# Layer 3's later keys and values moved behind the context pass, and the context's normed rows made by ScalarE and GpSimd

## The chip, the cores and the metric

One core of one Trainium2 chip runs the whole program. The metric is the device time of one execution in microseconds (us). Engines: PE is TensorE (matmul), PEld its weight loads, DVE is VectorE, ACT is ScalarE, POOL is GpSimd, SP is SyncE, which here only issues DMAs. A PE clock of 1.00 in the profile is the upper of TensorE's two levels (2.4 GHz), 0.50 the lower (1.2 GHz); a value between them is a mean over a stretch.

## The reference

Four layers of cross-attention and feed-forward act on x (8 batches of 56 tokens, width 128). Every layer but layer 2 attends with keys and values made from the same context, 8 batches of 1500 rows of 128:

```python
x = x + tanh(g_xattn[0]) * L0_xattn(layernorm(x), ctx, ctx, mask, ...)   # linear attention, 16 heads
x = x + tanh(g_ffn[0])   * L0_ffn(layernorm(x), ...)                      # ternary weights, int8-like rows
x = x + tanh(g_xattn[1]) * L1_xattn(layernorm(x), ctx, ctx, ...)          # window of 64
x = x + tanh(g_ffn[1])   * L1_ffn(...)                                    # 16 + 2 experts
x = x + tanh(g_xattn[2]) * L2_xattn(ctx, layernorm(x), ...)               # keys and values of layer_norm(ctx, w, b)
x = x + tanh(g_ffn[2])   * L2_ffn(...)
x = x + tanh(g_xattn[3]) * L3_xattn(ctx, ctx, layernorm(x), Wv, Wk, Wq)   # ctx @ Wk.T, ctx @ Wv.T
x = x + tanh(g_ffn[3])   * L3_ffn(...)                                    # 8 experts
```

Layer 0 needs, of each context batch, normed keys and scaled values; layer 2 needs the context's rows with their mean taken off, divided by their deviation, times a weight plus a bias (`L2_xattn_ln_x_w`, `L2_xattn_ln_x_b`); layer 3 needs plain products of the context with two 128x128 matrices. 1500 rows are 125 partitions times 12 tiles.

## The kernel before, in words

Each engine has its own program, written out in the order in which it runs; semaphores order them against one another, nothing else does. The program has stages, one after another.

**The context pass** (to 254.7 us) is eight turns of `context(b, p, ...)`, one function of that name for PE, ACT and DVE, with buffers p = b % 2. In a turn PE makes the centred rows (`cT` times `w_c`, L684), layer 3's keys (L692), layer 0's keys and values (L701), layer 0's sums over the batch before (`l0_sums`, L663), layer 3's values (L713), layer 2's keys of the batch before, for their norms (`l2_keys`, L673), and the turned normed rows (L726). DVE takes the centred rows out of PSUM, times the reciprocal deviation plus the bias, into `cln` (L1730); it makes the lower half of layer 3's keys (float16 remainders), key features (`key_features`, L1696), the statistics of the next batch (`statistics`, L1710 to L1719), sums of squares (L1749), the scaled keys `kn`, and layer 2's norms (`l2_norms`, L1702). ACT squares and copies PSUM banks. POOL multiplies `kn` by a weight and adds a bias (L1443, L1444) and makes `rhs0` out of the loaded rows (L1448 to L1452). SP stores `cln`, its turned form, and layer 3's keys and values of every batch to HBM (`store_results`), and loads the batch after next once `rhs0` is made.

**The middle** (254.7 to 339.7 us) is layer 0's attention on the sums of the pass, its dense layer, its feed-forward and the queries of layer 1; it ends where DVE first reads layer 1's scores (`shift1(0)`). It is a chain of small steps. Where PE would idle, `keep_clock(n, bank)` (L645) issues n matmuls that nobody reads. DVE sums and rounds the five ternary weight matrices there (`weight_sums`, `quantised_weights`). A `layernorm` on DVE waits in its middle for POOL (`rsqrt`, L1462), which raises four numbers per row to the power -0.5.

**After it** come layer 1's attention and experts, layer 2 (460 to 615 us; POOL adds up probabilities at L1521 all along), its feed-forward, layer 3 and its experts. The change leaves their order alone except where it says so.

The helper `tt` on DVE is `tensor_tensor` and has line L1551 wherever it is called from.

```python
dve.tensor_scalar(kpr, kn, 0.0, 1e-6, ALU.max, ALU.add).then_inc(l0_kp, 1)   # key_features, L1696
```

## Time and profile before

| | us |
|---|---|
| three runs | 911.19, 912.78, 916.82 (median 912.78) |
| profiled execution | 915.11 |
| its span, first to last instruction | 913.5 |

The span holds the context pass (0 to 254.7), the middle (254.7 to 339.7), and the rest. In the page of the profile "busy" is the time in which an engine executed something; the timeline views give start and length of instructions that follow one another with one form (xN: so many), and in brackets the idle time before them with the engine that ended it. A length includes a wait that the engine makes after it has begun an instruction.

### The profile page before, as it was taken

How to read it: one execution, taken by the hardware profiler on the slowest of the kernel's cores; microseconds unless marked ns; L12 is line 12 of the kernel's file. 1: busy time of each engine (PE TensorE's matmuls, PEld its weight loads, DVE VectorE, ACT ScalarE, POOL GpSimd, SP SyncE). 2: the span in 40 equal slices, each digit the busy share in tenths (PEclk: the TensorE clock that was granted, in tenths of full speed). 3: DMA queues.
4: the chain of work that ended last, by engine and by line, in shares of the span. 5: the costliest groups of instructions: out<-in, count | busy, mean ns of one | idle time of the engine just before them, and what ended most of it. 6: DMA issues, size and time to landing. Idle time of an engine off the chain costs nothing.

```text
span 913.5 us, 16850 instructions
## 1 busy us (share of the span) xinstructions
PE 803.2 (88%) x5836; PEld 513.8 (56%) x5836; DVE 632.3 (69%) x1302; ACT 396.7 (43%) x650; POOL 278.0 (30%) x215
## 2 busy tenths in 40 slices
PE   4879998899877877899789999998889999988996
PEld 3757776677644435566345555555326656654665
DVE  4869989697779768465645566557788988806652
ACT  1556665566620203253344554540016766663341
POOL 2431344313413012045147777770050000000111
PEclk9889999899998898699989999999958998999999
DMA  6467766564232000020602242205804455500230
GB/s 187 153 223 250 262 218 198 200 202 162 85 120 21 1 1 1 1 74 32 160 1 71 85 120 74 70 0 69 167 2 117 123 135 156 156 2 24 70 104 22
DMA packets 46651, 94.03 MB, mean 103 GB/s; under 512 B 16698, under 2 KB 30010, under 8 KB 44274
## 3 DMA queue, kind: packets, MB, share of 16 engines
q1 hardware_dynamic: 46594, 93.25, 34.9%
q8 instruction: 38, 0.62, 0.3%
q14 instruction: 19, 0.16, 0.1%
HBM read 61.58 MB, written 31.65 MB: 102 GB/s over the span
## 4 chain that ended last, share of the span: by engine, by line
PE 38%; DVE 22%; issue 4%; ACT 3%; POOL 3%; DMA 1%; POOLq 0%; DVEq 0%; ACTq 0%
DVE arena L2099 9%; PE ps L997 8%; PE ps L987 6%; DVE arena L1551 4%; PE ps L930 2%; PE ps L1164 2%; PE ps L1174 2%; PE ps L1099 2%; PE ps L1088 2%; ACT arena L1382 2%; POOL arena L1521 2%; PE ps L943 1%; PE ps L1073 1%; POOL arena L1462 1%; PE ps L879 1%
## 5 line engine op out<-in xcount | busy, mean ns | idle before, releaser
L1551 DVE TENSOR_TENSOR arena<-ps,arena 128x448 f32<-128x448 f32 (+8 forms) x160 | 99.2, 641 | 65.3 <-ACT arena L1405 19.1
L2099 DVE TENSOR_REDUCE arena<-ps 112x1 f32<-112x500 f32 x192 | 115.6, 667 | 18.3 <-PE ps L1073 17.4
L1521 POOL TENSOR_TENSOR arena<-arena 125x448 f32<-125x448 f32 x96 | 108.8, 1133 | 26.3 <-ACT arena L1359 24.8
L1382 ACT ACTIVATE arena<-ps 125x896 f32<-125x896 f32 x96 | 87.0, 917 | 30.4 <-PE ps L1088 29.9
L997 PE MATMUL ps<-arena 125*128 125x448 f32 (+1 forms) x208 | 98.3, 554 | 1.3 <-ACT arena L1359 0.8
L1462 POOL TENSOR_TENSOR arena<-arena 112x4 f32<-112x4 f32 x11 | 11.3, 1025 | 287.5 <-DVE arena L1575 281.4
L1551 DVE TENSOR_TENSOR arena<-ps,rn 125x448 f32<-125x448 f32 x96 | 59.3, 618 | 51.3 <-PE ps L987 47.0
L1359 ACT ACTIVATE arena<-arena,kbias 125x448 f32<-125x448 f32 x96 | 63.7, 668 | 66.7 <-DVE arena L1551 46.3
L645 PE MATMUL ps<-w_k2h 128*128 128x512 f16 x376 | 88.7, 391 | 0.4 <-ACT arena L1285 0.4
L673 PE MATMUL ps<-w_k2h,arena 128*125 128x512 f16 x288 | 70.1, 401 | 12.5 <-ACT arena L1245 12.3
L987 PE MATMUL ps<-arena 128*125 128x448 f16 (+3 forms) x312 | 78.1, 360 | 3.0 <-DVEq L1562 3.0
L1443 POOL TENSOR_TENSOR arena<-arena,vec 125x1536 f32<-125x1536 f32 x8 | 27.7, 3458 | 154.9 <-DVE arena L1551 154.9
L987 PEld LDWEIGHTS ps<-arena 128*125 128x125 f16 (+1 forms) x312 | 40.8, 135 | 57.8 <-issue 42.6
L1702 DVE TENSOR_REDUCE rn<-arena 125x512 f32 (+1 forms) x96 | 61.0, 681 | 5.8 <-ACT arena L1213 5.8
L1213 ACT ACTIVATE arena<-ps 125x512 f32<-125x512 f32 x96 | 57.3, 597 | 16.8 <-PE ps L673 13.1
L645 PEld LDWEIGHTS ps<-w_k2h 128*128 128x128 f16 x376 | 37.5, 101 | 45.8 <-issue 7.4
L1496 POOL TENSOR_TENSOR arena<-arena 112x512 f32<-112x512 f32 x26 | 32.9, 1265 | 95.5 <-DVE arena L1551 95.1
L673 PEld LDWEIGHTS ps<-w_k2h,arena 128*125 128x125 f16 x288 | 40.7, 144 | 37.3 <-ACT arena L1245 13.6
L1073 PE MATMUL ps<-arena 64*112 64x500 f16 x192 | 55.2, 450 | 7.1 <-issue 4.3
L1099 PE MATMUL ps<-arena 125*32 125x168 f32 x768 | 51.9, 342 | 8.7 <-ACT arena L1382 8.3
L997 PEld LDWEIGHTS ps<-arena 125*128 125x128 f32 (+1 forms) x208 | 38.3, 192 | 14.0 <-issue 8.4
L1088 PE MATMUL ps<-arena 64*125 64x112 f16 x768 | 43.6, 242 | 0.0
(278 smaller groups left out, 1403.4 us busy)
## 6 DMA issues: line engine op xcount, KB each, us to landing
d_k<-arena SPq DMA_DIRECT2D x24, 375.0 KB
d_v<-arena SPq DMA_DIRECT2D x8, 1125.0 KB
arena<-d_k SPq DMA_DIRECT2D x96, 93.8 KB
arena<-d_v SPq DMA_DIRECT2D x8, 1008.0 KB
arena<-in_ctxT SPq DMA_DIRECT2D x8, 750.0 KB, 14.1
d_cln<-arena SPq DMA_DIRECT2D x8, 750.0 KB
d_clnT<-arena SPq DMA_DIRECT2D x8, 750.0 KB
arena<-d_clnT SPq DMA_DIRECT2D x8, 750.0 KB
```

The costliest lines, as they stand in the source:

```text
L645: pe.matmul(ps[0:D, k, :], w_k2h[:, 0, 0:D], w_k2h[:, 0, :], start=True, stop=True)
L673: mm = pe.matmul(ps[0:KP, k, :], clnT[p][:, a, KP * j:KP * j + KP], w_k2h[:, w, :], start=(n == 0), stop=(n == 2))
L987: mm = pe.matmul(ps[0:rows, (t + p) % 2, 0:N].rearrange("p (h q) -> p h q", h=H8), clnT_s[p][:, a, cols:cols + rows], qtT[:, q, :, bass.ds ...
L997: pe.matmul(ps[0:D, 4 + 2 * p, 0:N], cln_s[p][0:rows, t, :], pexp[(t + p) % 2][0:rows], start=(t == 0), stop=(t == KT)).then_inc(l2_pv, 1)
L1073: pe.matmul(ps[0:TT, max_bank(bn, u), 0:500], q.rearrange("p o h q -> p (o h q)"), kst[pn][64 * r:64 * r + 64, g, 500 * third:500 * third ...
L1088: mm = pe.matmul(ps[0:KP, 2 * (t % 2) + r, 112 * g:112 * g + 112], kst[p][rows, g, KP * t:KP * t + KP], qst3[rows, b:b + 1, g, 2 * r:2 * r ...
L1099: pe.matmul(ps[32 * g:32 * g + 32, 6, 0:168], v3s[p][:, t, 32 * g:32 * g + 32], p3[t % 2][:, 3 * g:3 * g + 3, :].rearrange("p h q -> p (h ...
L1359: act.activation(pexp[(t + p) % 2][0:rows], sscl[(t + p) % 2][0:rows], ACT.Exp, bias=bias)\
L1382: act.activation(p3[t % 2].rearrange("p (k h) q -> p k (h q)", k=2), ps[0:KP, 2 * (t % 2):2 * (t % 2) + 2, 0:8 * S], ACT.Exp).then_inc(l3_ ...
L1521: ins = pool.tensor_tensor(psum2[p][0:rows], psum2[p][0:rows], pexp[(t + p) % 2][0:rows], ALU.add)
L1551: return dve.tensor_tensor(out, a, b, op)
L2099: dve.tensor_reduce(mx3[bn % 2][:, u % 2, u % 8 // 2, u // 8:u // 8 + 1], ps[0:TT, max_bank_of(bn, u), 0:500], AX.X, ALU.max).then_inc(l3_ ...
```

## The change

It does eight things.

1. The centring product goes: `w_c`, its 12 matmuls a turn on PE and the 12 DVE instructions that read them. Instead ACT makes the normed rows from the loaded ones with 12 instructions of 125x128 (`rows`: a scale and a bias per row, which DVE's new `scales` makes), at the end of the turn before; POOL multiplies them by the weight and adds the bias (two 125x1536 instructions).
2. Of layer 3's keys and values each turn makes the first third (a "unit": 500 keys, 4 tiles of values). The other 16 units, numbered 8 to 23, are made in the middle: `later(...)` on PE and ACT, `remainders(...)` on POOL, `store_later` and `load_later` on SP.
3. POOL makes the keys' lower halves (`late_k` minus the upper half) and a second copy of the upper half. POOL's turn is now: normed rows, remainder, `rhs0`, `kn`.
4. Layer 0's query path (layernorm of x, product with `w_q0`, layernorm, turn) moves from the middle to the start of the program, as `query_rows`, `query_norm`, `query_columns`.
5. The last batch's layer 2 keys, squares and norms move from the end of the pass into the middle, into the time in which layer 0's attention is stored and loaded again.
6. The `keep_clock` calls of the middle are replaced by units, or go. Layer 0's hidden banks shrink from eight to six to make room.
7. Three of the five ternary matrices are rounded where all five were; the other two between the first two batches of layer 2.
8. The loops of the pass are written out. The loads of layer 2's weights and of the first experts come later; DVE waits for the last stores of units ahead of `shift1(0)`.

```diff
+UNITS = [(b, 0) for b in range(B)] + [(b, third) for b in (7, 6, 0, 1, 2, 3, 4, 5) for third in (1, 2)]
...
@@ SP @@
+            def store_later(u):
+                (b, third), h = UNITS[u], u % 3
+                sp.wait_ge(l_lo, u + 1)
+                sp.wait_ge(l_dup, u + 1)
+                sp.dma_start(k3_in[b, :, :, 500 * third:500 * third + 500], late_k3[h]).then_inc(st_l[h], 16)
...
@@ PE context @@
-                for u in range(3):
-                    k = bank_d(b, u)
-                    for j in range(4):
-                        mm = pe.matmul(ps[0:KP, k, D * j:D * j + D], cT[p][:, 4 * u + j, :], w_c,
-                                       start=True, stop=True)
...
+                later_keys(cT[p][:, 0:4, :], bank_a(b, 6)).then_inc(a_full, 1)
+                later_values(cT[p][:, 0:4, :], bank_a(b, 7)).then_inc(a_full, 1)
...
@@ PE middle @@
+            def later(*units):
+                for u in units:
...
+                    if u > B:
+                        pe.wait_ge(lk_taken, u - B)
+                    later_keys(tiles, 6).then_inc(lk_full, 1)
+                    if u > B:
+                        pe.wait_ge(lv_taken, u - B)
+                    later_values(tiles, 7).then_inc(lv_full, 1)
...
-            keep_clock(45, 3)
+            later(10, 11)
+            pe.wait_ge(l0_att, 1)
+            l2_keys(B, 1, 0, bank=3)
...
@@ ACT @@
+            def take_later(u, k, keys, values):
...
+                if u:
+                    act.wait_ge(l_lo, u)
+                act.wait_ge(*keys)
+                act.copy(late_k3[h][:, 0, :], ps[0:D, k[0], 0:500])
+                act.copy(late_k, ps[0:D, k[0], 0:500]).then_inc(keys_taken(u)[0], 1)
...
+            def rows(b, p, loads):
+                act.wait_ge(st[p], 32 * loads)
+                act.wait_ge(c_rstd, b + 1)
+                for j in range(KT):
+                    ins = act.activation(cln[p][:, j, :], c_in[p][:, j, :], ACT.Identity, bias=sm[:, 12, j:j + 1],
+                                         scale=sm[:, 6, j:j + 1])
+                ins.then_inc(c_rows, 1)
...
@@ POOL @@
+            def remainders(*units):
+                for u in units:
+                    k3 = late_k3[u % 3]
+                    pool.wait_ge(*keys_taken(u))
+                    pool.tensor_tensor(k3[:, 1, :], late_k, k3[:, 0, :], ALU.subtract).then_inc(l_lo, 1)
+                    pool.tensor_copy(k3[:, 2, :], k3[:, 0, :]).then_inc(l_dup, 1)
+
+            for b in range(B):
+                p = b % 2
+                pool.wait_ge(c_rows, b + 1)
+                ch.link(pool.tensor_tensor(cln[p], cln[p], spread("L2_xw", KP, KT), ALU.mult))
+                pool.tensor_tensor(cln[p], cln[p], spread("L2_xb", KP, KT), ALU.add).then_inc(c_ready, 1)
+                remainders(b)
+                pool.wait_ge(l0_w, b + 1)
+                pool.wait_ge(acc_full, b + 1)
+                ch.step(pool.tensor_copy(rhs0[:, :, D:D + 1], em[:, b, :].unsqueeze(2)))
+                ch.step(pool.tensor_copy(rhs0[:, :, D + 1:D + 2], em2[:, b, :].unsqueeze(2)))
+                pool.tensor_tensor(rhs0[:, :, 0:D], c_in[p], sm[:, 11, 0:KT].unsqueeze(2)
+                                   .broadcast_to([KP, KT, D]), ALU.mult).then_inc(l0_rhs, 1)
+                pool.wait_ge(l0_kn, b + 2)
+                ch.link(pool.tensor_tensor(kn, kn, spread("L0_g", KP, KT), ALU.mult))
+                pool.tensor_tensor(kn, kn, spread("L0_b", KP, KT), ALU.add).then_inc(l0_kaff, 1)
...
@@ DVE @@
+            def scales(b):
+                dve.wait_ge(c_sd, b + 1)
+                ch.link(dve.reciprocal(sm[:, 6, 0:KT], sm[:, 5, 0:KT]))
+                tt(sm[:, 12, 0:KT], sm[:, 3, 0:KT], sm[:, 6, 0:KT], ALU.mult).then_inc(c_rstd, 1)
...
-                for j in range(KT):
...
-                    ins = dve.scalar_tensor_tensor(cln[p][:, j, :], ps[0:KP, 3 + j // 4, D * (j % 4):D * (j % 4) + D],
...
-                    tt(k_lo[p][:, 500 * u:500 * u + 500], ps[0:D, 3 + u, 0:500],
-                       k_hi[p][:, 500 * u:500 * u + 500], ALU.subtract).then_inc(d_free, 1)
...
+            for h in range(3):
+                dve.wait_ge(st_l[h], 32 * 8)
             shift1(0)
...
             batch2(0, 0, first=True)
+            quantised_weights((3, 4))
             batch2(1, 1)
```

What the engines' programs say now, at the places that matter. First POOL, one turn of the pass before (`kn` times weight, plus bias, then `rhs0`):

```order
L1443 TENSOR_TENSOR arena<-arena,vec 125x1536
L144 REGISTER_ALU
L1444 TENSOR_TENSOR arena<-arena,vec 125x1536
L1448 ISA
L1448 COPY arena<-em 125x12
L1450 REGISTER_ALU
L1450 COPY arena<-em 125x12
L1452 TENSOR_TENSOR arena<-arena 125x12x128
```

And the same turn of POOL after the change (L1584 and L1585 are the normed rows, L1578 and L1579 the remainder and the second copy, L1589 to L1591 `rhs0`, L1594 and L1595 `kn`):

```order
L1584 TENSOR_TENSOR arena<-arena,vec 125x1536
L1585 TENSOR_TENSOR arena<-arena,vec 125x1536
L1578 TENSOR_TENSOR arena<-arena 128x500
L1579 COPY arena<-arena 128x500
L1589 COPY arena<-em 125x12
L1590 COPY arena<-em 125x12
L1591 TENSOR_TENSOR arena<-arena 125x12x128
L1594 TENSOR_TENSOR arena<-arena,vec 125x1536
L1595 TENSOR_TENSOR arena<-arena,vec 125x1536
```

POOL's turn grew from three long instructions to six, and `kn` went from the first place to the last.

PE in the middle before, from the rotation of layer 1's keys (L775) to the products of the feed-forward (L809); L645 is `keep_clock`:

```order
L775 MATMUL ps<-arena,cst 128x448
L777 MATMUL ps<-mw,cst 128x5
L645 MATMUL ps<-w_k2h 128x512 x45
L631 MATMUL ps<-cst,arena 128x112 x4
L645 MATMUL ps<-w_k2h 128x512 x8
L637 MATMUL ps<-w_d,arena 112x128 x4
L789 MATMUL ps<-vec,cst 56x512 x2
L794 MATMUL ps<-arena 56x64 x16
L645 MATMUL ps<-w_k2h 128x512 x32
L804 MATMUL ps<-ident_h,arena 128x112 x4
L809 MATMUL ps<-wquant,arena 112x512 x8
```

The same stretch after it, as far as the dense layer (L698), where L738 and L743 are the keys and values of a unit (10, 11 and 12) and L781 the last batch's layer 2 keys:

```order
L854 MATMUL ps<-arena,cst 128x448
L856 MATMUL ps<-mw,cst 128x5
L738 MATMUL ps<-arena,w_k 128x500
L743 MATMUL ps<-w_v,arena 125x128 x4
L738 MATMUL ps<-arena,w_k 128x500
L743 MATMUL ps<-w_v,arena 125x128 x4
L781 MATMUL ps<-w_k2h,arena 125x512 x36
L692 MATMUL ps<-cst,arena 128x112 x4
L738 MATMUL ps<-wex,w_k 128x500
L743 MATMUL ps<-w_v,wex 125x128 x4
L698 MATMUL ps<-w_d,arena 112x128 x4
```

Work that is needed stands where the filler stood; four more units come before L804's successor.

POOL around the two layernorms of the middle before (L1476 builds layer 1's key blocks, L1462 is `rsqrt`, once for the dense layer's rows, once for the feed-forward's, once for layer 1's):

```order
L1462 TENSOR_TENSOR arena<-arena 112x4
L1476 TENSOR_TENSOR arena<-arena,cst 128x16x56 x4
L1462 TENSOR_TENSOR arena<-arena 112x4 x3
L1476 TENSOR_TENSOR arena<-arena,cst 128x16x56 x4
L1462 TENSOR_TENSOR arena<-arena 112x4
```

And after it, from the second key block (L1613; L1562 is `rsqrt`) on, down to the third of seven remainders that follow the second `rsqrt`:

```order
L1613 TENSOR_TENSOR arena<-arena,cst 128x16x56 x2
L1578 TENSOR_TENSOR arena<-arena 128x500
L1579 COPY arena<-arena 128x500
L1562 TENSOR_TENSOR arena<-arena 112x4
L1578 TENSOR_TENSOR arena<-arena 128x500
L1579 COPY arena<-arena 128x500
L1562 TENSOR_TENSOR arena<-arena 112x4
L1578 TENSOR_TENSOR arena<-arena 128x500
L1579 COPY arena<-arena 128x500
L1578 TENSOR_TENSOR arena<-arena 128x500
L1579 COPY arena<-arena 128x500
```

Each `rsqrt` stands behind remainders now, and POOL, idle before, works beside the DVE chain.

## Rows read from the trace of the kernel before

**Rows 1.** Busy time by stage: start:end, length, PE, PEld, DVE, ACT, POOL, PEclk, DMA, GB/s

```profile
46.00:236.00 190.00, 173.27 (x999) 132.87 (x998) 158.94 (x358) 115.05 (x254) 65.19 (x32) 0.96 0.62 210
254.75:339.67 84.92, 68.43 (x374) 36.06 (x374) 64.06 (x165) 10.06 (x13) 14.22 (x14) 0.92 0.17 38
460.00:615.00 155.00, 151.88 (x534) 81.76 (x534) 89.65 (x143) 75.90 (x111) 116.02 (x104) 0.98 0.21 62
```

**Rows 2.** Timeline of DVE: start, length, instructions; sums of squares (turns 1, 6, 7), one wait

```profile
54.21 3.35 DVE L1749 TENSOR_REDUCE arena<-arena 125x24 f32<-125x3072 f32 x1
...
165.32 2.42 DVE L1710 BATCH_NORM_STATS2 arena<-arena 125x6 f32<-125x128 f32 x12 [4.48 <-DMA arena<-in_ctx]
...
197.95 3.35 DVE L1749 TENSOR_REDUCE arena<-arena 125x24 f32<-125x3072 f32 x1 [0.64 <-ACT arena L1230]
...
223.94 3.35 DVE L1749 TENSOR_REDUCE arena<-arena 125x24 f32<-125x3072 f32 x1 [3.92 <-ACT arena L1230]
```

**Rows 3.** Timeline of DVE: parts of turn 6 from the reciprocal to the norms

```profile
186.89 0.22 DVE L1725 RECIPROCAL arena<-arena 125x12 f32<-125x12 f32 x1
...
193.08 0.95 DVE L1696 TENSOR_SCALAR arena<-arena 125x1536 f32<-125x1536 f32 x1
...
196.39 0.36 DVE L1551 TENSOR_TENSOR arena<-arena 125x12 f32<-125x12 f32 x3
...
201.46 0.29 DVE L1691 COPY kv_all<-ps 128x130 f32 x1
...
202.34 1.75 DVE L1551 TENSOR_TENSOR arena<-arena 125x1536 f32<-125x1536 f32 x1
204.07 3.92 DVE L1702 TENSOR_REDUCE rn<-arena 125x512 f32 x6
```

**Rows 4.** Timeline of POOL, turn 6

```profile
204.18 3.48 POOL L1443 TENSOR_TENSOR arena<-arena,vec 125x1536 f32<-125x1536 f32 x1 [19.37 <-DVE arena L1551]
207.73 3.45 POOL L1444 TENSOR_TENSOR arena<-arena,vec 125x1536 f32<-125x1536 f32 x1
...
211.40 2.76 POOL L1452 TENSOR_TENSOR arena<-arena 125x1536 f32<-125x1536 f32 x1
```

**Rows 5.** Timeline of ACT: a copy of 125x128, turn 6

```profile
202.03 0.27 ACT L1245 COPY arena<-ps 125x128 f32<-125x128 f32 x1
```

**Rows 6.** Timeline of DVE and POOL at the end of the pass and in layer 1's attention

```profile
239.09 1.75 DVE L1696 TENSOR_SCALAR arena<-arena 125x1536 f32<-125x1536 f32 x1
...
237.26 2.76 POOL L1452 TENSOR_TENSOR arena<-arena 125x1536 f32<-125x1536 f32 x1
...
342.19 2.07 DVE L1551 TENSOR_TENSOR arena<-arena 128x1024 f32<-128x1024 f32 x1
...
359.07 1.23 DVE L1551 TENSOR_TENSOR arena<-arena 128x1024 f32<-128x1024 f32 x1
...
341.48 4.32 POOL L1476 TENSOR_TENSOR arena<-arena,cst 128x896 f32<-128x896 f32 x2
```

**Rows 7.** Groups of POOL by form: count, busy us, mean ns

```profile
L1521 POOL TENSOR_TENSOR arena<-arena 125x448 f32<-125x448 f32 x88 | 99.8, 1134 | 23.0 <-ACT arena L1359 21.5
...
L1531 POOL TENSOR_TENSOR arena<-arena,gm 128x896 f16 x8 | 13.1, 1679 | 9.6 <-DVEq L1562 9.6
```

**Rows 8.** Timeline of DVE in the middle

```profile
255.19 0.87 DVE L1567 BATCH_NORM_STATS2 arena<-x 112x6 f32<-112x128 f32 x4
...
259.57 1.22 DVE L1795 COPY arena<-ps 128x1024 f32<-128x1024 f32 x1
...
267.77 0.62 DVE L1599 COPY arena<-ps 128x448 f32<-128x448 f32 x1
...
275.88 2.81 DVE L1638 TENSOR_REDUCE mw<-arena 128x5 f32<-128x2560 f32 x1
...
284.88 7.58 DVE L1654 TENSOR_SCALAR arena<-arena,wscale 128x512 f32<-128x512 f32 x5
292.49 1.50 DVE L1657 TENSOR_SCALAR arena<-arena 128x2560 f32<-128x2560 f32 x1
```

464 lines of the change are left out of this document (274 added, 190 removed).

## The prediction

> **What bounds the kernel now.** I read the busy time by stage first [rows 1]. In turns 1 to 7 of the pass PE is busy 173.3 of 190 us and DVE 158.9: two engines near their limit, while ACT has 115.1 and POOL 65.2. Then the place of one instruction that stands once in each turn, DVE's sum of squares [rows 2]: 197.95 to 223.94 is a turn of 26.0 us with nothing late; the mean from turn 1 to turn 7 is (223.94 - 54.21) / 6 = 28.3, and the rest are waits for loads, such as the 4.48 us at 165.32. Last, what DVE and POOL do to each other [rows 6]. The key features L1696 take 0.95 us where POOL is idle [rows 3], but 1.75 us at 239.09: POOL's instruction runs to 240.02, and DVE's ends 0.82 us after that. The subtraction at 342.19, both of whose inputs lie in SBUF, takes 2.07 us against 1.23 at 359.07; POOL works beside the first and not beside the second. The five roundings from 284.88 take 7.58 us [rows 8], though at the rate of the one behind them (1.50 us for 2560 columns) they need 0.3 us each: each waits for one of POOL's key block instructions. DVE and POOL thus take turns wherever DVE needs what POOL needs. In the pass this costs next to nothing today, since POOL is busy for 10 us of a turn, and DVE is then at reductions and at instructions that read PSUM, which show no delay: the six reductions at 204.07 take 3.92 us beside POOL [rows 3].
>
> The Trainium skill (SBUF — State Buffer, "Who interferes with whom") says the same as a rule: a pair of ports is shared between VectorE and GpSimd, held for a whole instruction, and needed by VectorE's copies and tensor_scalars in fast modes and by instructions with two SBUF inputs while GpSimd reads. The trace agrees, with the 2.07 against 1.23 us. The rule speaks against this change; for 12-column instructions, no row shows it.
>
> **The pass, by sums of busy time.** PE has 23.7 us of work in a turn of 26 (173.3 / 190 of it) and loses 12 centring, two key and eight value products: it no longer bounds. DVE loses the stretch from its reciprocal at 186.89 to the key features at 193.08 [rows 3], 12 reads of PSUM and three remainders: 6.2 us, of a turn in which it hardly stands, so 20 stay. ACT has 15.7 us a turn; it gives back some copies of keys and values, about what its new key copy costs, and gets 12 instructions of 125x128. No row shows one with a scale and a bias per row: the copy of that size takes 0.27 us [rows 5], of which 0.16 passes before the next starts, so 12 cost 1.9 to 4 us; I take 2.6, since they stand back to back. POOL gets two 125x1536 instructions, at the 3.5 us each of [rows 4], and a 128x500 remainder. That one is bounded by 1679 x 500/896 = 0.94 us and 1134 x 500/448 = 1.27 [rows 7]; I take 1.26, its f32 input being like the latter's; and its copy, which no row shows, lies between 0.2 (a 12-column copy) and 1.26: I take 0.6. If only these sums counted, a turn would take 20 to 21 us, bound by DVE, and by ACT with its waits for the sum of squares.
>
> **The pass, with turns taken.** The longest ring of a turn runs through POOL and DVE alternately. From the release of `rhs0`: `rhs0` with its copies 3.04; `kn` 6.94 (204.18 to 211.12); the first instruction on the normed rows 3.5. DVE's key features have been waiting for `kn`, then wait for that one: 0.9. The second normed-row instruction 3.4; behind it DVE's small statistics with two SBUF inputs, 0.9 (three of eight take 0.36); sum of squares and scalar 3.51 (197.95 to 201.46); reciprocals 0.88; scaled keys 1.73 [rows 3, 4]. The sum is 24.8 us, against 26.0 now.
>
> The start is later, by an estimate: the query path waits for x (about 11.5 us, with the first loads); a layernorm without its rows takes 2.7 (4.4 from 255.19 to 259.57, less 1.7 for the rows [rows 8]), the context's statistics and scale 4.9, ACT's rows 2.7, PE and a copy 2, the second layernorm 2.7: 26.5. Then DVE's small statistics of batch 1 wait behind POOL: three query instructions of 112x512 (1.3 each by the rate of 1134 ns for 448) and both on the normed rows, to 38.5. The sum of squares follows; turn 1's sum of squares then starts 25.7 later, at 64.6, where it is 54.21 today. Five turns of 24.8 give 188.6, and turn 7, without statistics, 20.6: 209.2, against 223.94. From there to the end of the pass: 3.51 + 0.88 + 1.73 + 3.04 + 6.94 + 0.86 + 2.9 for the last sums + 0.5 of latencies = 20.4, since the last norms (8 us) have left for the middle. That is 229.6; I add 3.4 for loads still late, a third of the 10 us of today, as the loads go out 11 us ahead now instead of 6. So 233.0 against 254.7: **-21.7**.
>
> **The middle.** Removed: layernorm and rows of x from 255.19 to the copy at 259.57 (3.6 us of it on the chain) and the query steps from 267.77 to 275.88 [rows 8]: -11.7. Added:
> - Sixteen units. POOL works 1.86 us for each; one unit follows another in about 2.5 us (ACT's two key copies, estimated at 1.1, POOL's remainder 1.26, latencies), 40 us in all, for which the 85 have room. But 14 of the 16 fall beside chains of small DVE instructions that need what POOL holds: the scaling of layer 0's matrices (8, 9), the layernorms (13 to 16, 20 to 22), the roundings (12, 17 to 19). Where DVE's step is short and POOL has the next ready, each POOL instruction is waited for once. I take 1.4 us of the 1.86 for each, +19; the bounds are 5 (one in four met) and 26 (all in full).
> - The last batch's norms: 12 x 0.65 + 0.45 = 8.3 on DVE. They lie beside the store and load of layer 0's attention, but the rounding stands behind them: it falls from 10.6 us to about 5. +2.7.
> - DVE's wait for the stores of unit 23 ahead of `shift1(0)`: +1.8. Behind it are queued all of layer 1's attention on DVE and, for their banks, PE.
> - No filler. PE's clock reads 0.92 in this stage [rows 1]; the chain has some 12 us of PE in it, and gaps without filler will put part of it at the lower level: +2.
>
> Sum **+13.8**: the middle takes 99 us instead of 85.
>
> **Layer 2.** Two matrices are rounded between batches 0 and 1: 2.1 us of DVE, each of its four instructions behind one of POOL's 1134 ns additions [rows 7], 6.6 in all. PE, busy 151.9 of 155 us, runs two tiles ahead and feels **+3** of it (bounds 0 and 6.6). The later loads of the experts (behind unit 23, some 45 us ahead of their use) and of layer 2's weights are hidden behind layer 1's attention; if that cover went they would cost some 14 us.
>
> The sum: -21.7 + 13.8 + 3 = -4.9, so the profiled execution goes from 915.1 to 910.2. It stands 2.3 above the median of the three runs; the median goes from 912.8 to **908**.
>
> **Rivals.**
> - Turns are taken as said in the pass, but hardly in the middle: units cost 6 instead of 19, because DVE's short instructions slip in between POOL's. 908 - 13 = 895. For it: PE had filler there, and POOL's 14 us in 85 leave room. Against it: the roundings at 284.88 met POOL every time.
> - Only the sums count, in both: a turn of 21.5 and a pass that ends near 200, with no cost in the middle beyond the fill: about 862. [Rows 6] are against it.
> - Slower: `rsqrt` stands in POOL's order behind remainders, and a remainder waits for ACT's copy, and that for PE. If a unit is late when a layernorm asks for its power, DVE stands for the unit's whole 2.5 us plus its own turn-taking, and PE cools. Place: the three `rsqrt` of the middle and the fourteen units around them; price 1.3 us more for each of 14, 18 in all: 926. It decides from 0.35 us a unit above my count, where the time before is reached, and is over 1% slower from 1.0 us on.
> - The waits for loads stay as they are: with 10 us of them instead of 3.4, 915. For it: stores of small pieces (1000 bytes a row) are added to SP's queue. Against it: a turn moves 3.75 MB instead of 5.25.
>
> **How the numbers follow.** About 1% (9 us) is what a measurement of this kernel can tell from no change; the three runs span 0.6%. My forecast 0.40, its own range 898 to 918, of it 0.09 faster, 0.28 within, 0.03 slower; first rival 0.25, faster; second 0.04, faster; slower rival 0.18; loads 0.13, of it 0.10 within and 0.03 slower. Sums: 0.38 faster, 0.38 within 1%, 0.24 slower. The range 888 to 926 reaches into the first and third rival and leaves 0.2 out.
>
> **What would show each step.** A turn of 24 to 26 us between DVE's sums of squares, with key features of over 4 us that end just after POOL's instruction; POOL busy 19 us a turn; PE idle for 5 us or more of each turn. A turn below 22 would prove the ring wrong, one above 27 that something else is in it. The pass's end at 230 to 237. In the middle, DVE's 112x128 and 112x512 instructions lengthened by 0.6 to 1.3 us beside POOL, and 95 to 103 us for the stage; below 85 would favour the first rival, above 110 the slower one. PE's clock below 0.85 there by more than a few us of chain would show that the filler was worth more than I took.

## The result and the profile after

| | before | after |
|---|---|---|
| runs, us | median 913.0 of 4 (911.19 to 916.82) | median 927.86 of 4 (925.74 to 930.52) |
| profiled execution, its span, us | 915.11, 913.5 | 926.91, 925.1 |

The ratio is 1.016, with a 95% interval of 1.012 to 1.020: the change made the kernel slower by 15 us. The prediction was 908, with a range up to 926. One mark on DVE's timeline cuts the execution in the same places in both: the memset of 128x32 that follows the last sums of the pass, and the first instruction on layer 1's scores (`shift1(0)`).

| stretch | before | after | difference | predicted |
|---|---|---|---|---|
| context pass, to the memset | 255.06 | 232.69 | -22.4 | -21.7 |
| middle, memset to `shift1(0)` | 84.6 | 116.7 | +32.1 | +13.8 |
| the rest | 573.8 | 575.7 | +1.9 | +3 |

So two of the three terms came out within 1.1 us, and a miss of 18 us lies in the middle. First the pass, in DVE's timeline of the kernel after (start, length, instruction, in brackets the idle time before it). It answers to [rows 2, 3]:

```profile
110.81 3.35 DVE L1887 TENSOR_REDUCE arena<-arena 125x24 f32<-125x3072 f32 x1
...
115.08 1.75 DVE L1694 TENSOR_TENSOR arena<-arena 125x1536 f32<-125x1536 f32 x1
116.75 0.22 DVE L1869 RECIPROCAL arena<-arena 125x12 f32<-125x12 f32 x1
117.01 2.75 DVE L1694 TENSOR_TENSOR arena<-arena 125x12 f32<-125x12 f32 x1
...
128.55 0.95 DVE L1840 TENSOR_SCALAR arena<-arena 125x1536 f32<-125x1536 f32 x1
...
132.52 2.77 DVE L1860 TENSOR_SCALAR arena<-arena 125x12 f32<-125x12 f32 x1
...
135.56 3.34 DVE L1887 TENSOR_REDUCE arena<-arena 125x24 f32<-125x3072 f32 x1
```

A turn is 135.56 - 110.81 = 24.75 us, where 24.8 was predicted. But the key features (L1840) take 0.95 us, not over 4. What is long are two instructions of 12 columns, 2.75 and 2.77 us, where such an instruction needs 0.17, as before the change:

```profile
33.19 0.17 DVE L1551 TENSOR_TENSOR arena<-arena,em 125x12 f32<-125x12 f32 x1
```

POOL's timeline shows what they wait for:

```profile
116.98 2.75 POOL L1591 TENSOR_TENSOR arena<-arena 125x1536 f32<-125x1536 f32 x1
119.69 3.44 POOL L1594 TENSOR_TENSOR arena<-arena,vec 125x1536 f32<-125x1536 f32 x1
123.22 3.44 POOL L1595 TENSOR_TENSOR arena<-arena,vec 125x1536 f32<-125x1536 f32 x1
128.70 3.57 POOL L1584 TENSOR_TENSOR arena<-arena,vec 125x1536 f32<-125x1536 f32 x1 [2.04 <-ACT arena L1323]
132.35 2.91 POOL L1585 TENSOR_TENSOR arena<-arena,vec 125x1536 f32<-125x1536 f32 x1
```

The instruction at 117.01 ends at 119.76, when `rhs0` (L1591) has ended at 119.73; the one at 132.52 ends at 135.29, after POOL's L1585 at 135.26. No bracket stands at either, and the page counts both as busy DVE: a wait for the other engine is hidden inside an instruction's length.

Now the middle. These are DVE's instructions with the long waits, and the two marks:

```profile
232.69 0.09 DVE L1942 MEMSET arena<- 128x32 f32 x1 [0.36 <-DVE kv_all L1835]
...
293.34 0.39 DVE L1986 COPY arena<-ps 128x448 bf16<-128x448 bf16 x1 [8.45 <-PE ps L886]
...
309.48 0.39 DVE L1775 COPY arena<-ps 128x448 bf16<-128x448 bf16 x1 [4.78 <-PE ps L905]
...
320.39 1.11 DVE L1730 TENSOR_SCALAR arena<-x,arena 112x128 f32<-112x128 f32 x4 [3.67 <-POOL arena L1562]
334.88 0.62 DVE L1742 COPY arena<-ps 128x448 f32<-128x448 f32 x1 [13.37 <-PE ps L692]
...
349.37 1.23 DVE L1694 TENSOR_TENSOR arena<-ps,cst 128x1024 f32<-128x1024 f32 x1 [8.15 <-DMA d_v<-arena]
```

The last two, before the change:

```profile
332.23 0.62 DVE L1599 COPY arena<-ps 128x448 f32<-128x448 f32 x1 [0.78 <-PE ps L631]
...
339.67 1.23 DVE L1551 TENSOR_TENSOR arena<-ps,cst 128x1024 f32<-128x1024 f32 x1 [2.06 <-PE ps L862]
```

In three of the five waits the releaser named is PE, but PE was late itself. The groups of waits of this stretch (who waited for what: us in total, times, longest) say for what:

```profile
PE ps L738 <- DMA wex<-in_ctxT: 25.3, 4, 9.7
ACT arena L1385 <- PE ps L839: 14.9, 1, 14.9
DVE arena L1742 <- PE ps L692: 13.4, 1, 13.4
...
DVE arena L1694 <- DMA d_v<-arena: 8.2, 1, 8.2
ACT arena L1298 <- DMA d_v<-arena: 7.8, 4, 2.7
```

L738 makes a unit's keys; it waits four times for the turned context that `load_later` brings, and `transposes(z)` (L692), which DVE needs, is queued behind it in PE's order. The chain of waits has three of these four transfers and one of the last stores (start, length):

```profile
277.56 11.58 DMA wex<-in_ctxT
...
302.39 12.00 DMA wex<-in_ctxT
315.51 15.24 DMA wex<-in_ctxT
...
341.39 7.79 DMA d_v<-arena
```

Five hundred KB take 12 us here. Before, the DMA engines were almost at rest in the middle (a share of 0.17 in [rows 1]); now the share is above a half, PE's granted clock is lower and POOL has three times the work (start:end, length, PE, PEld, DVE, ACT, POOL, PEclk, DMA share, GB/s):

```profile
232.69:349.37 116.68, 71.28 (x370) 47.97 (x369) 62.68 (x142) 42.77 (x88) 44.93 (x46) 0.82 0.54 149
```

### The profile page after: what moved, and what is told of

Its sections match the earlier page's. It is cut to its first block, busy times and chain, and to the rows that moved or that the text cites. A ratio compares the mean times of both kernels' runs of the same rounds, so it can differ in the third digit from the quotient of the medians.

```text
span 925.1 us, 15643 instructions
## 1 busy us (share of the span) xinstructions
PE 754.9 (82%) x5460; PEld 485.1 (52%) x5460; DVE 624.3 (67%) x1177; ACT 447.6 (48%) x782; POOL 385.7 (42%) x285
## 4 chain that ended last, share of the span: by engine, by line
PE 40%; DVE 34%; ACT 8%; DMA 7%; POOL 6%; issue 4%; SPq 1%; DVEq 0%; POOLq 0%; ACTq 0%
DVE arena L2252 9%; DVE arena L1694 8%; PE ps L1078 7%; PE ps L1068 6%; DMA wex<-in_ctxT 4%; DVE rn L1846 3%; DVE arena L1887 2%; PE ps L1011 2%; PE ps L1246 2%; PE ps L1256 2%; PE ps L1181 2%; PE ps L1170 2%; ACT arena L1323 2%; ACT arena L1505 1%; POOL arena L1664 1%
## 5 line engine op out<-in xcount | busy, mean ns | idle before, releaser
L1694 DVE TENSOR_TENSOR arena<-ps,arena 128x448 f32<-128x448 f32 (+8 forms) x136 | 82.9, 634 | 58.7 <-ACT arena L1528 19.4
L1562 POOL TENSOR_TENSOR arena<-arena 112x4 f32<-112x4 f32 x9 | 9.2, 1027 | 228.7 <-DVE arena L1718 222.7
L795 PE MATMUL ps<-w_l,arena 128*125 128x256 f32 x192 | 58.7, 469 | 26.9 <-ACT arena L1353 26.9
L781 PE MATMUL ps<-w_k2h,arena 128*125 128x512 f16 x288 | 66.1, 380 | 4.7 <-ACT arena L1316 4.7
L795 PEld LDWEIGHTS ps<-w_l,arena 128*125 128x125 f32 x192 | 44.4, 237 | 39.3 <-ACT arena L1353 30.1
L1846 DVE TENSOR_REDUCE rn<-arena 125x8 f32<-125x512 f32 x96 | 58.6, 672 | 0.1
L1578 POOL TENSOR_TENSOR arena<-arena 128x500 f16<-128x500 f32 x24 | 28.4, 1184 | 70.8 <-ACT arena L1299 70.8
L1694 DVE TENSOR_TENSOR arena<-arena 125x12 f32<-125x12 f32 (+5 forms) x71 | 51.8, 747 | 1.4
L781 PEld LDWEIGHTS ps<-w_k2h,arena 128*125 128x125 f16 x288 | 38.1, 136 | 27.5 <-ACT arena L1316 8.8
```

What stands on the lines that cost most here:

```text
L781: mm = pe.matmul(ps[0:KP, k, :], clnT[p][:, a, KP * j:KP * j + KP], w_k2h[:, w, :], start=(n == 0), stop=(n == 2))
L795: mm = pe.matmul(ps[0:KP, k, 256 * j:256 * j + 256], cT[p][:, 2 * u + j, :], w_l0[:, :, :].rearrange("p a n -> p (a n)"), start=True, stop ...
L1694: return dve.tensor_tensor(out, a, b, op)
L1846: dve.tensor_reduce(rn[:, bass.ds(turn - 1, 1), j, :].rearrange("p o h -> p (o h)"), sqk[:, j % SQ, :].rearrange("p (h d) -> p h d", h=H8) ...
```

## The experiments

In all tables "middle" is the length between the two marks in the profiled execution. It is one reading per kernel, and executions of one kernel differ: the two of x5 took 896.3 and 900.3 us, the two of x7 883.7 and 889.4. A difference of a few us between two middles is therefore weak by itself. Unless said otherwise the edits are made to the changed kernel.

### Which of the new things in the middle costs what

**x1_no_reloads.**

```
-                if u in (13, 15, 17, 19):
-                    sp.wait_ge(lv_full, u - 7)
-                    load_later((u - 9) // 2)
...
-                        pe.wait_ge(ld_x[i % 2], 16 * (i // 2 + 1))
+                        pe.wait_ge(ld_x[i % 2], 16)
```

> The changed kernel without the four loads of turned context into wex for units 16 to 23 (the units are computed from the batches that already lie there, so layer 3's keys and values of batches 2 to 5 are left out of the computation). Theory (the middle is long because PE stands in its program order before units 16, 18, 20 and 22 until their load, about 12 us each, has landed): in the changed kernel DVE waits 8.45, 4.78, 3.67 and 13.37 us in the middle where the kernel before waits 0.54, 0.1, 1.12 and 0.78, so 24 to 27 us go and the time falls from 928 to about 903; the middle (117 us) to about 92. Rival (POOL's remainders and copies, by the port and by rsqrt standing behind them, are the cost of the middle, as the prediction took, 19 us): the loads only fill waits that would be there anyway, and the time falls by less than 8 us, to 920 or more.

Measured: 921.8 us, middle 107.8. 6 us went, 8.9 of the middle. That is the rival's number (less than 8), but what it named as the cause, POOL, isn't what is waited for: the loads' waits went, and waits for stores came. The groups of waits of the middle:

```profile
ACT arena L1295 <- DMA d_v<-arena: 26.2, 8, 4.8
DVE arena L1691 <- DMA d_v<-arena: 14.2, 1, 14.2
```

ACT may not write a unit's buffer before the stores of three units earlier have landed, and it now waits for them 8 times. Loads were only what stood in front.

**x2_scores_moved.**

```
+        at[0] = big2_at
         sc1 = [carve([D, 16, SP]) for _ in range(2)]
         pr1 = [carve([D, 16, SP]) for _ in range(2)]
...
+            for h in range(3):
+                act.wait_ge(st_l[h], 32 * 8)
...
-            for h in range(3):
-                dve.wait_ge(st_l[h], 32 * 8)
             shift1(0)
```

> The changed kernel with layer 1's scores and probabilities in memory that the units don't use (that of big2 and big3), so that DVE's wait for the stores ahead of shift1(0) goes; ACT waits for them instead ahead of its first copy of turned probabilities, some 10 us later. Theory (the store of unit 23 is the last to land, 7.8 us after its issue, and DVE's first instruction on the scores waits 8.15 us for it where the kernel before waits 2.06): 6 us go, 928 to 922. Rival (unit 23 itself and PE's scores end hardly earlier, or the store is waited for elsewhere at once): under 2 us, 926 or more.

Measured: 917.5 us, middle 109.3 (7.3 less). The theory's mechanism holds, with 7 us in the middle for 6; the time fell by 10.

**x3_small_remainders.**

```
+                    n = 500 if u < B else 8
-                    pool.tensor_tensor(k3[:, 1, :], late_k, k3[:, 0, :], ALU.subtract).then_inc(l_lo, 1)
-                    pool.tensor_copy(k3[:, 2, :], k3[:, 0, :]).then_inc(l_dup, 1)
+                    pool.tensor_tensor(k3[:, 1, 0:n], late_k[:, 0:n], k3[:, 0, 0:n], ALU.subtract).then_inc(l_lo, 1)
+                    pool.tensor_copy(k3[:, 2, 0:n], k3[:, 0, 0:n]).then_inc(l_dup, 1)
```

> The changed kernel with POOL's remainder and second copy cut from 500 to 8 columns for the units 8 to 23 (the rest of these keys' lower parts is left out of the computation), so that POOL's 1.75 us for each of 16 units nearly go. Theory (in the middle the lengthened DVE instructions sum to some 5 to 7 us and POOL's late rsqrt to 1 or 2, the loads are what counts): 3 to 6 us go, part of it hidden by the loads, 928 to about 924. Rival (the prediction's term of 1.4 us for each of 14 units, 19 us, is the cost of the middle): 928 to about 909.

Measured: 923.3 us, middle 112.9 (3.8 less): as the theory said. As long as transfers are waited for, most of POOL's cost is hidden in them.

**x5_small_stores, x6_small_stores_no_reloads, x7_no_dma_small_remainders.** The second has the edits of x1 too, the third those of x1 and x3.

```
+                nk, nv = (D, KP) if u < B else (8, 8)
-                sp.dma_start(k3_in[b, :, :, 500 * third:500 * third + 500], late_k3[h]).then_inc(st_l[h], 16)
+                sp.dma_start(k3_in[b, 0:nk, :, 500 * third:500 * third + 500], late_k3[h][0:nk]).then_inc(st_l[h], 16)
...
-                sp.dma_start(batch(d_v3, b)[:, 768 * third:768 * third + 768],
-                             late_v[h].rearrange("p j d -> p (j d)")).then_inc(st_l[h], 16)
+                sp.dma_start(batch(d_v3, b)[0:nv, 768 * third:768 * third + 768],
+                             late_v[h][0:nv].rearrange("p j d -> p (j d)")).then_inc(st_l[h], 16)
...
```

> The changed kernel with the stores of units 8 to 23 cut to 8 of 128 rows (the other rows of layer 3's keys and values of these thirds are filled from other memory during layer 2, so most of these stores' data is left out); the four loads of turned context stay. What is read is the middle, from DVE's memset of 128x32 to its first instruction on layer 1's scores: 116.7 us in the changed kernel; the time itself also carries the filling. Without the loads alone the middle was 107.8, and ACT then waited 26 us for stores and DVE 14. Theory A (the middle is bound by the DMA traffic of its units, 0.75 MB of stores each and 2 MB of loads, and the loads are slow, 12 us for 0.5 MB, because they share the engines with the stores): the loads take about 5 us instead of 12, DVE's wait ahead of the scores falls to 2, and the middle to about 95. Theory B (the loads' own dependence on the unit before is what counts and the stores matter only at the end): loads stay at 10 to 12 us and the middle is about 108 to 110.

> The two edits together: stores of units 8 to 23 cut to 8 of 128 rows, and no loads of turned context for units 16 to 23 (the same parts of layer 3's keys and values are left out as in each alone). Theory A (DMA traffic, both halves): all waits for transfers but the two of layer 0's attention go, and the middle falls to 80 to 88 us, that is, to what the kernel before needs (84.6) or a little less; the store and load of layer 0's attention take less than their 11.8 us. Rival (the chain of ACT's copies, POOL's remainder and PE for each unit, 2.5 us a unit as the prediction took, is itself a bound): the middle stays at 95 or more.

> As the kernel with small stores and no loads, and also with POOL's remainders and second copies of units 8 to 23 cut from 500 to 8 columns (left out besides). With the traffic out of the way this shows POOL's own cost in the middle. Theory (lengthened DVE instructions and late rsqrt, 4 to 7 us by the trace of the changed kernel): the middle is 4 to 7 us shorter than with full remainders. Rival (the prediction's 1.4 us for each of 14 units): 15 to 20 us shorter.

| | time, us | middle, us |
|---|---|---|
| after | 927.9 | 116.7 |
| x1: no loads | 921.8 | 107.8 |
| x5: small stores | 898.3 | 90.5 |
| x6: both | 895.3 | 87.8 |
| x7: both, small remainders | 886.5 | 77.7 |

Theory A held in x5 (90.5, even below its 95) and in x6 (87.8 in 80 to 88). The loads alone cost 90.5 - 87.8 = 2.7 us, less than executions of x5 differ by; what made them late was the company of the stores: without these they land in a median of 3.5 us instead of 11.9. POOL's own cost is 87.8 - 77.7 = 10.1 us, between the two expectations (4 to 7, 15 to 20). DVE's busy time shows where it sits; of x6 and x7:

```profile
232.13:319.90 87.77, 66.68 (x370) 44.12 (x369) 66.48 (x142) 42.62 (x88) 42.92 (x45) 0.90 0.19 34
```

```profile
232.74:310.40 77.66, 63.48 (x370) 42.73 (x369) 55.52 (x141) 42.45 (x88) 19.18 (x45) 0.93 0.23 43
```

DVE is busy for 11.0 us less with one instruction fewer in the window. With full and with small remainders, the same DVE instructions:

```profile
279.00 2.46 DVE L1740 TENSOR_SCALAR arena<-x,arena 112x128 f32<-112x128 f32 x4 [2.72 <-POOL arena L1572]
...
283.32 2.10 DVE L1772 TENSOR_SCALAR arena<-arena 112x128 f32<-112x128 f32 x4
```

```profile
275.04 1.11 DVE L1741 TENSOR_SCALAR arena<-x,arena 112x128 f32<-112x128 f32 x4 [1.38 <-POOL arena L1572]
...
277.80 0.87 DVE L1773 TENSOR_SCALAR arena<-arena 112x128 f32<-112x128 f32 x4
```

1.35 and 1.23 us more, and 1.34 of waiting for a `rsqrt` that stands behind a remainder.

### What makes the stores slow

**z1_key_stores_cut, z2_value_stores_cut.** As x5, for the keys alone (`nv = KP`) and for the values alone (`nk = D`).

> The changed kernel with only the stores of the keys of units 8 to 23 cut to 8 of 128 rows (375 KB each in 384 pieces of 1000 bytes; filled from other memory during layer 2), values and loads as they are. With both stores cut the middle was 90.5 instead of 116.7 us, 26 less. Theory (the number of short pieces is what makes the stores slow): keys alone give 20 us or more of the 26, the middle is 92 to 97. Rival (bytes, or the time of one store in the chain of its buffer, the value's store being the last of the two): keys alone give 8 to 14, the middle is 103 to 109.

> The changed kernel with only the stores of the values of units 8 to 23 cut to 8 of 125 rows (375 KB each in 125 pieces of 3072 bytes), keys and loads as they are. Theory (short pieces): 2 to 6 us less, the middle at 111 to 115. Rival (bytes, each half alike): 12 to 18 us less, the middle at 99 to 105.

Measured: without the keys' stores 913.4 us, middle 100.1 (16.6 less); without the values' 897.5 us, middle 86.3 (30.4 less). All four expectations fail: the values, with the same bytes in a third as many pieces, cost nearly twice as much. The two don't add up either: without both (x5) the middle was 90.5. The last store ahead of `shift1(0)` in the chain of waits, first with only the values' stores whole, then with only the keys':

```profile
322.05 9.64 DMA d_v<-arena
```

```profile
316.39 3.01 DMA d_v<-arena
```

375 KB of values land 9.64 us after their issue, though hardly any keys are stored beside them. In the other kernel the keys' 375 KB were issued at 315.81 and 24 KB of values at 316.39, and both have landed at 319.40, 3.6 us after the first. The two aren't quite alike: the trace's records of single packets show that the packets of the store issued at 322.05 began only at about 325, when those of the store before it (issued at 317.83) were through, and the load of an expert ran beside them. That the values' stores stand in line behind one another is itself the finding, and z1 has a stretch in which hardly anything else moves (the last three numbers are granted clock, DMA share, GB/s):

```profile
318.00:320.00 2.00, 1.54 (x10) 0.82 (x8) 0.42 (x1) 1.95 (x5) 0.84 (x1) 1.00 0.34 97
```

A share of 0.34 of 16 DMA engines is between 5 and 6 of them, and they move 97 GB/s. The candidates left are the shape, 125 rows against 128, and the length of a piece.

**z3_value_stores_split.** Nothing left out.

```
-                sp.dma_start(batch(d_v3, b)[:, 768 * third:768 * third + 768],
-                             late_v[h].rearrange("p j d -> p (j d)")).then_inc(st_l[h], 16)
+                for rows in (slice(0, 112), slice(112, KP)):
+                    sp.dma_start(batch(d_v3, b)[rows, 768 * third:768 * third + 768],
+                                 late_v[h][rows].rearrange("p j d -> p (j d)")).then_inc(st_l[h], 16)
```

> The changed kernel, nothing left out, with one edit: each unit's store of values (125 rows of 3072 bytes) is issued as two, of 112 and 13 rows, as the kernel does for its loads of context. With the value stores cut the middle was 86.3 us and the last store landed in 3.0 us; with the key stores cut it was 100.1 and the last value store took 9.6 us for 375 KB alone. Theory (a transfer of 125 rows is carried by a few of the 16 DMA engines only, one of 112 rows by all): the value stores land in 3 to 5 us, the loads between them in 4 to 6 instead of 12, and the middle falls to 88 to 95 us, the time to 898 to 907. Rival (the values' bytes or their 3072-byte pieces are slow in themselves): no change, 926 to 930.

Measured: 903.1 us, ratio to the kernel before 0.985 (0.980 to 0.990), middle 92.7. As the theory said: one edit takes 25 us off, and the changed kernel becomes the faster of the two. Bytes and piece length are the same as before the edit, so the rival falls. Of the chain's last store and DVE's wait behind it:

```profile
321.97 3.08 DMA d_v<-arena
```

```profile
325.24 1.23 DVE L1695 TENSOR_TENSOR arena<-ps,cst 128x1024 f32<-128x1024 f32 x1 [4.10 <-DMA d_v<-arena]
```

The second piece of the values' store lands 3.08 us after its issue and the whole 3.7 us after the first piece's issue at 321.32, and the loads of turned context in a median of 5.3 instead of 11.9. The Trainium skill (DMA: Bandwidth & Descriptors, "Why a DMA increments its semaphore by 16 and not by 1") says that a transfer issued from SP runs on the largest number of DMA engines, up to 16, that divides its rows: 5 for 125 rows, 16 for 112 or 128. The trace agrees. Only the values' stores of units move in packets of 3072 bytes, and of these no more than 5 are at work at once in 97% of the time in which any are (the kernel after, packet records); in z3 it is up to 16. The packets of one such store take 3.4 us or more in z1 and 1.5 us or more with the split.

The same records show what bound the middle. In the kernel after, the 14 values' stores of units 10 to 23 keep these five engines at work from 264.7 to 348.8 us with gaps of 0.6 us in all, one store in 6.0 us; in z3 such packets are in flight for 27.6 of the 61.6 us from the first to the last. It also explains the loads: a load spread over all engines has its share on the five where the values' stores stand queued. Of the 128 packets of the load issued at 315.51, 95 had ended by 321.9, and the last of the other 33 ended at 330.4.

### What sets the turn of the pass

**x4_pass_order.** DVE's 12-column instructions stand elsewhere: the small statistics of the next batch behind the sum of squares, its scales ahead of the release of `rhs0`.

```
                 dve.tensor_scalar(sm[:, 7, :], sm[:, 10, :], 1.0 / D, 1e-6, ALU.mult, ALU.add)\
                     .then_inc(l0_var, 1)
+                if more:
+                    moments(b + 1)
...
                 ch.link(dve.reciprocal(sm[:, 9, :], sm[:, 8, :]))
+                if more:
+                    scales(b + 1)
...
                 tt(kn, kraw, r[:, :, 0:1].broadcast_to([KP, KT, D]), ALU.mult).then_inc(l0_kn, 1)
-                if more:
-                    scales(b + 1)
```

> The changed kernel with two groups of DVE's 12-column instructions moved in each turn of the pass: the small statistics of the next batch from ahead of the sum of squares to behind it, and the scales of the next batch from behind the scaled keys to ahead of the release of POOL's rhs0; ACT takes the deviation after the square root of the sums. Nothing is left out. Theory (DVE is busy 24.45 of the 24.75 us of a turn, of which 2.6 and 2.6 us are one 12-column instruction each that waits until POOL's long instruction has ended): the turn falls until the next bound, ACT's chain of squares, copies and rows of about 23.5 us, is met, so 1 to 3 us a turn in seven turns, 928 to about 915. Rival (the ring through POOL and DVE drawn in the prediction, rhs0, kn, the normed rows in alternation with DVE, sets the turn of 24.8): the turn stays within 0.3 us and the time within 2 us, 926 to 930.

Measured: 927.3 us. A turn is 24.17 us: 0.58 less, between the two expectations, and the time is the rival's. DVE's waits in its instructions are gone, its busy time in a turn is 19.00 instead of 24.45, and the time came back as a wait for ACT:

```profile
134.88 3.35 DVE L1889 TENSOR_REDUCE arena<-arena 125x24 f32<-125x3072 f32 x1 [4.00 <-ACT arena L1353]
```

The 2.5 us that the pass gained were lost in the middle (118.6), whose transfers landed no earlier.

**p0_half_rows, p1_half_rows_pass_order.** ACT makes half of its rows, in the changed kernel and in x4.

```
-                for j in range(KT):
+                for j in range(KT if b < 2 else KT // 2):
```

> The changed kernel with ACT making 6 instead of 12 of the normed rows of batches 2 to 7 (the other half of these rows is left out; POOL still works on all of them). ACT has 2.35 us less in six turns. Theory (the turn of 24.75 us is DVE's own work, 24.45 us busy, of which two 12-column instructions of 2.75 us wait for POOL's port): the turns change by less than 0.6 us and the time by less than 3 us. Rival (ACT's chain of squares, copies and rows sets the turn already in the changed kernel): 2 us a turn, 12 us.

> The same half of ACT's rows left out, in the version with DVE's 12-column instructions moved (its turn is 24.17 us, in which DVE waits 4.0 us for ACT). Theory (in that version ACT is the bound: from the square root of the sums on, 6 squares, 3 copies, 6 squares, 12 rows and 12 squares and copies stand back to back): the six turns lose 1.8 to 2.4 us each and become 21.8 to 22.4 us. Rival (the ring of the prediction through POOL's and DVE's alternating instructions sets it): the turns stay at 24 us.

Measured: p0 has turns of 22.98 us, 1.77 less: the theory falls. Two sums of squares of p0:

```profile
84.89 3.35 DVE L1887 TENSOR_REDUCE arena<-arena 125x24 f32<-125x3072 f32 x1
...
107.87 3.35 DVE L1887 TENSOR_REDUCE arena<-arena 125x24 f32<-125x3072 f32 x1
```

p1 has turns of 22.5 on the mean ((194.90 - 82.58) / 5), 1.7 less: ACT's chain, a little less than was expected. p1's time is 908.4; p0's two executions took 904.7 and 921.7 (the profiled one), too far apart for a time to be read. So although DVE was busy for 24.45 of 24.75 us, ACT's work set the turn: DVE's instruction waited for POOL's, and POOL's for ACT's rows.

**q1_short_bias.**

```
+                n = KT if b < 1 else 1
-                pool.tensor_tensor(cln[p], cln[p], spread("L2_xb", KP, KT), ALU.add).then_inc(c_ready, 1)
+                pool.tensor_tensor(cln[p][:, 0:n], cln[p][:, 0:n], spread("L2_xb", KP, n), ALU.add).then_inc(c_ready, 1)
```

> The changed kernel with POOL's second instruction on the normed rows (the bias) cut to one of 12 tiles for the batches 1 to 7 (the rest of the bias is left out), so that POOL has about 2.7 us less in each of seven turns. The ring as the prediction drew it (rhs0, kn and both normed-row instructions back to back on POOL, DVE in between): the turn falls by the 3.4 us of that term, 24.75 to about 21.4. The ring as the trace of the changed kernel shows it (DVE's sum of squares 3.5, ACT's square root, squares, copies and rows 14.2, POOL's two instructions 6.6 with DVE's 12-column instruction waiting for the second, then the sum of squares again) is tied with ACT's own chain of 24.17 us, as the version with DVE's instructions moved showed: the turn falls by no more than 0.6 us, to 24.1 or 24.2.

Measured: 922.8 us, turns of 24.08 us ((180.90 - 60.52) / 5). The ring of the prediction alone would have given 21.4; ACT's chain, at 24.17 in x4, would have stopped it there in any case, so q1 shows only a bound near 24.1 in which this instruction has no part. The run that speaks against the ring is p0. The turn of the changed kernel goes through ACT: DVE's sum of squares (110.81 to 114.40 with what follows), ACT's squares, copies and rows (to 128.62), POOL's two instructions (to 135.26), 0.3 to the next sum. ACT's rows in it:

```profile
123.91 4.71 ACT L1323 ACTIVATE arena<-arena 125x128 f32<-125x128 f32 x12
```

### Versions with nothing left out

**y1_buffers_scores** has x2's edit and memory of their own for three of the four loads; layer 2's weights are loaded behind unit 23:

```
+                dst = more_cT[i - 2] if 2 <= i < 5 else wex[i % 5][:, 500:C]
...
+            sp.wait_ge(rn_sq, 1)
+            for i in range(2, 5):
+                load_later(i)
```

> The changed kernel with nothing left out: the turned context of batches 2, 3 and 4 is loaded into memory of its own (that of the squares, once they are done) at once after layer 0's attention is loaded, batch 5 once wex is read; layer 2's weights are loaded behind unit 23; and layer 1's scores and probabilities lie outside the units' buffers. Theory A (DMA traffic of the middle counts): the waits for loads go, but ACT's waits for the stores of three buffers take their place as they did without loads; DVE's wait ahead of the scores goes; the middle is 98 to 103 us and the time 909 to 914, 4 to 8 us below the version with the scores moved alone (917.5). Rival (only the loads' dependence on the unit before counts): the middle is 86 to 92 and the time 898 to 903.

Measured: 909.3 us, middle 90.5. The time is theory A's, the middle the rival's: the stores were waited for behind the mark (ACT stood 11.94 us for them ahead of its first copy of turned probabilities, and DVE 12.75 us behind it).

**y3_all_moved, y4_all_moved_pass** move those probabilities too, into the memory of the hidden rows (`pT1`), and y4 adds x4's edit.

> Nothing left out: the version with loads into memory of their own and the scores moved, and now layer 1's turned probabilities too lie outside the units' buffers (in that of the hidden rows), so that nothing in layer 1's attention waits for stores; POOL waits for them ahead of its memset of layer 2's queries. Theory (in the version before it ACT's first copy of turned probabilities still waited for the last stores, seen as DVE's 12.75 us wait at 350.52, 8 us more than in the changed kernel): 7 to 8 us go, 909 to 901 or 902. Rival (the traffic of the last stores delays the loads of the first experts, queued behind them, which are waited for instead): under 3 us.

> As the last, with DVE's 12-column instructions moved in the pass. In the changed kernel this move took 2.5 us off the pass (232.7 to 230.2) but left the time where it was, as the middle then waited that much longer for its transfers. Theory (with no such waits left, the 2.5 us stay): 2 to 3 us below the last, 898 to 900. Rival (transfers still bound the middle): no difference.

Measured: 907.9 and 906.4 us, each from 10 runs that spread over some 12 us. y3 gave less than 3 us, as its rival said. Its middle is 101.0 in the profiled execution, which was the slowest of its ten, and y4's is 99.9, with 33 us in which ACT waited for stores: now the transfers are waited for ahead of the mark, not behind it. That this is what ate the gain is read from the waits and was not tried by itself. The 1.5 us between them can't be told from nothing. They beat the kernel before by 0.5 and 0.65%.

**y5_dup_by_dma, y6_full_split.** y5 is y4 with the second copy made by a second store instead of by POOL; y6 is y5 with the split of z3.

```
-                    pool.tensor_copy(k3[:, 2, :], k3[:, 0, :]).then_inc(l_dup, 1)
...
-                sp.dma_start(k3_in[b, :, :, 500 * third:500 * third + 500], late_k3[h]).then_inc(st_l[h], 16)
+                sp.dma_start(k3_in[b, :, 0:2, 500 * third:500 * third + 500], late_k3[h][:, 0:2]).then_inc(st_l[h], 16)
+                sp.dma_start(k3_in[b, :, 2:3, 500 * third:500 * third + 500], late_k3[h][:, 0:1]).then_inc(st_l[h], 16)
```

> The last full version (own memory for the loads, scores and turned probabilities outside the units' buffers, DVE's 12-column instructions moved), and the second copy of the keys' upper half is no longer made by POOL: SP stores the upper half twice. The same bytes leave; POOL has 0.6 us less for each of 24 units, SP one issue more. Theory (POOL's 10 us in the middle with the traffic out of the way were 0.35 by the copy, but the traffic is what is waited for in a full version): 0 to 2 us below 906.4. Rival (POOL's chain for each unit still counts, as the late rsqrt of 3.7 and the waits of 7.7 us in that version could be read): 3 to 5 us less, 902 to 903.

> The best full version so far (902.5 us) with the same split of the value stores. In it ACT waits 27 us for stores in the middle, 10 times. Theory (rows of 125 on few engines): these waits go almost wholly, the middle falls from 93.0 to 82 to 86 us and the time to 892 to 896. Rival (bytes or pieces): 901 to 904.

Measured: 902.5 us (ratio 0.989, 0.984 to 0.995), middle 93.0, and 892.4 us (ratio 0.979, 0.975 to 0.982), middle 84.0. y5's 3.9 us less than y4 is the rival's number, but its six executions spread over 12 us and y4's ten over 12 too, so that it isn't shown. y6 came out as the theory said, and is faster than both kernels: 20 us below the one before. Its group of ACT's waits for stores, against y5's:

```profile
ACT arena L1315 <- DMA d_v<-arena: 2.1, 1, 2.1
```

```profile
ACT arena L1314 <- DMA d_v<-arena: 26.9, 10, 4.6
```

Its middle takes what the kernel before took (84.6), with sixteen units in it and the query path out of it.

## Why the prediction was wrong

**The pass: right sum, wrong ring.** Predicted -21.7, measured -22.4, with a turn of 24.75 for 24.8 and turn 7 at 209.57 for 209.2. Inside the sum two misses cancel: turn 1 starts at 61.32 instead of 64.6, and the turn that ends in turn 7 takes 24.07 (185.50 to 209.57) instead of 20.6. The ring that gave 24.8 isn't the one that runs. It had POOL working without a gap from `rhs0` to the end of the normed rows, with DVE's key features waiting; POOL in fact stands for 2.04 us before the rows, and the key features slip into that gap. The reason is a term taken too small: ACT's 12 rows at 2.6 us (bounds 1.9 to 4) took 4.71, above both bounds, and their place behind ACT's squares brought ACT into the ring, which the prediction had left beside it. That the two rings agree is chance; p0 shows that the predicted one doesn't set the turn: nothing in it was shortened, and the turn fell to 22.98. Of the signs, POOL's 19.5 us a turn came, PE stood 3.95 us a turn instead of 5 or more. (The items given for the start add up to 37.3 where 38.5 was taken, and 14 times 1.4 to 19.6 where 19 was; neither moves the result.)

**The rule on DVE and POOL held further than its rows.** The prediction said that no row shows it for 12-column instructions. Now rows do: 2.75 us for 0.17, and in x6 0.47 for 0.17 with 4 columns.

**The middle: the failed step.** It priced the sixteen units by their engines ("one unit follows another in about 2.5 us ... 40 us in all, for which the 85 have room") and their transfers by one term, the wait for the stores of unit 23, +1.8. The runs split the 116.7 us into 77.7 (x7) + 10.1 for POOL (x6 - x7) + 28.9 for transfers (after - x6):

| | predicted | measured |
|---|---|---|
| the rest: 84.6 less the query path, plus norms and clock | 84.6 - 11.7 + 2.7 + 2 = 77.6 | 77.7 |
| POOL beside DVE | 19 | 10.1 |
| transfers of the units | 1.8 | 28.9 |

The split depends on the order in which things are left out: beside the transfers POOL's remainders cost 3.8 us (x3), without them 10.1. The first line came out as a sum; no run tries its terms one by one, and the 2 us in it for the clock don't show in x7 (0.93, where 0.92 stood before). POOL's turn-taking costs half of what was taken; the bounds (5 and 26) held it. The transfers are the miss, 27 us. The prediction asked whether loads of the experts were hidden and whether the pass's loads were late, but not how long one unit's stores take, nor that with three buffers ACT stands until the stores of three units earlier have landed. In the pass that never mattered, with one unit in 24.75 us; in the middle a unit was to follow in 2.5 and followed in 6.0, the pace of the values' stores. A sum of bytes would not have warned of it: 12 MB of stores and 2 MB of loads in 85 us are 165 GB/s, and [rows 1] has 210 at a DMA share of 0.62. What was missing is that half of these stores have 125 rows and run on 5 of the 16 engines (z3).

**The rivals.** The slower one gave 926, close to 927.9, by another mechanism: it had DVE stand for `rsqrt` behind remainders, of which one wait of 3.67 us is seen. Less turn-taking (the first rival) did happen, 10.1 us for 19, and was covered by the transfers. Loads that stay late were a rival, but of the pass.

**Layer 2.** +3 was predicted for the two matrices rounded later; everything from `shift1(0)` on took +1.9. No run tries this term by itself.

**The clock.** It read 0.82 in the middle instead of 0.92. With the transfers' waits gone (x7, y6) it is back at 0.93 and 0.94 without any filler: the clock follows the waits, and needs no filler where units come without them. One place did lose by the missing filler: right after the first mark, where 18 filler products stood before, 16 products of 128x128 took 3.61 us (granted clock 0.53) for 2.05 (1.00).

## What to carry to other kernels

Work that is moved takes its transfers along: price a moved piece by the time for which its transfers hold the DMA engines that they run on, and by the round trip of its buffer (write, store, landing) divided by the number of buffers, and not only by its compute engines. (More buffers were not tried.) When a trace shows busy time of close to 100% of a turn, look for short instructions with long durations before calling that engine the bound: the wait for another engine can be inside. And split a transfer whose number of rows has no large divisor: here 125 rows became 112 and 13, and one such line was worth 25 us, more than the change itself had won in the pass. The stores of `cln` (L525, 125 rows of 6144 bytes) have the same shape: in the pass their packets too are 5 at a time, for some 7 us a turn, and no run split them.
